# A delta-rule scan in chunks: the step's VectorE work replaced by precomputed transitions, and the tail moved into its own turn

## The chip, the cores and the metric

One core of a Trainium2 chip. The metric is the device time of one execution in microseconds (us), lower is better. TensorE (PE) multiplies, VectorE (DVE) and ScalarE (ACT) do the elementwise work, GpSimd (POOL) helps, SyncE (SP) issues most transfers. Each engine runs its own program in order and waits on semaphores for the others.

## The reference

`x` is [8, 256, 256] (batch, time, hidden), float32. It goes through a gated delta-rule attention layer with a residual and a layer norm, then through one ternary product with a residual and a layer norm:

```python
q = causal_dwconv_silu(x @ Wq.T, conv_wq).reshape(B, T, H, DK)      # H, DK, DV = 6, 32, 64
k = causal_dwconv_silu(x @ Wk.T, conv_wk).reshape(B, T, H, DK)      # depthwise, 4 taps
v = causal_dwconv_silu(x @ Wv.T, conv_wv).reshape(B, T, H, DV)
beta = jax.nn.sigmoid(x @ Wb.T)
g = -jnp.exp(A_log) * jax.nn.softplus(x @ Wa.T + dt_bias)
q = l2norm(q) * DK ** (-0.5)
k = l2norm(k)
def step(S, inp):                                   # scanned over time
    S = S * jnp.exp(gt)[..., None, None]
    v_new = vt - jnp.einsum('bhk,bhkv->bhv', kt, S)
    S = S + bt[..., None, None] * (kt[..., :, None] * v_new[..., None, :])
    o = jnp.einsum('bhk,bhkv->bhv', qt, S)
...
o = rmsnorm(o) * norm_w * jax.nn.silu(x @ Wg.T)     # per head
x = _layernorm(x + o @ Wo.T)
x = _layernorm(x + ternary(x) @ (ternary(weight) + rram_variation).T)
```

## The kernel before

The eight sequences are done as four pairs (`PAIRS`), one pair a turn. A pair has 12 heads (6 of each sequence); a tensor of 128 partitions holds four of them, so a pair has three groups (`G3`). The 256 time steps are cut in 8 chunks (`NC`) of 32 (`CH`); a unit is one group and one chunk, 24 (`U`) in a pair. All small products go through `by_head` (line 327): four 32x32 products, one for each head of a group, on four quarters of TensorE. Each float32 product shows as two MATMUL and two LDWEIGHTS in the trace; below, a pair of instructions is one load with its matmul, so one call of `by_head` is 8 pairs of instructions.

What a turn `k` does, and who does it:

- Front of the next pair `k + 1`. Six projections `project` (lines 334 to 346, two 128x128x512 products of hidden size each), copied out of PSUM by ACT (`tile_out_of_psum`, 608), three taps of the convolution on DVE (`conv_taps`, 910), Silu on ACT (`silu`, 621). Then `kq_to_tokens` (922), `square` (ACT, 654), `factors` (943: sums of squares, a reciprocal square root by three Newton steps, and the scales), `scaled_operands` (960), `v_to_tokens` (929), `exponents` (PE, 360), `exp_d` (ACT, 647), the mask `d_masked` on POOL (850), `chunk_products` (PE, 370) and `chunk_matrices` (DVE, 984). The triangular 32x32 matrices of the units are inverted: their 16x16 halves by `substitute(j)`, `j` = 1 to 14 (1006), turned by `inverse_to_rows` (1016), then joined by two products, `merge` and `merge_second` (382, 392) with the copy `merge_out` (669) between them, and `inverse` (1024) writes the result `t_t`.
- The scan of pair `k`, chunk by chunk. `from_state` (400) multiplies the state with keys and queries, DVE adds the values (`residual`, 1048), `solve` (417) multiplies with the inverse, ACT copies the result `u_sb` out of PSUM (`u_out`, 684), `to_state` (429) makes the new state's part and the output's, POOL scales the old state (`decay_state`, 862) and DVE adds the two (`next_state`, 1056). So one step passes PE, DVE, PE, ACT, PE and DVE. The PE program of a turn (510 to 553) puts a piece of the front or of the tail between the pieces of a step, and the DVE program (1224 to 1288) and the ACT program (743 to 791) do the same.
- The heads' norm and gate of pair `k` (`head_norm`, 1067; `gated`, 1096), at the end of the turn, with the three gate projections (`gates`, 348).
- The tail of the pair before, `k - 1`: the output projection (`project_out`, 446), the residual (`attention_sum`, 1117), the first layer norm (`first_norm`, 1127, and `normalize` on ACT, 714), the ternary values (`ternary`, 1134), their transposes and products (`feed_forward`, 458; `feed_forward_products`, 467), `feed_forward_sum` (1143), `moments` (1103), the second `normalize` and the store (`store`, 303).

The last turn has no front; it has the tail of pair 2 and, after the scan, the tail of pair 3 in two halves (the functions with `end_`, 1153 to 1222). PSUM has eight banks: `pj` (2), `fr` (3), `pc`, `po`, `pg`. `pc` takes every product of the scan's step.

```python
for c in range(NC):                       # DVE, lines 1226 to 1285, cut
    residual(k, c)
...
    next_state(k, c)
```

## Time and profile before

| | us |
|---|---|
| runs | 401.51, 403.58, 404.87, median 403.58 |
| the profiled execution | 404.34 |
| its span in the profile | 402.6 |
| DVE busy | 295.6 (73%) |
| PE busy | 260.4 (65%) |
| ACT busy | 131.7 (33%) |
| POOL busy | 33.1 (8%) |

The span runs from the first to the last instruction; what lies around it is the difference to the execution's time, 1.7 us. Busy time of PE is that of matmuls in a pipeline. Line numbers are those of the kernel above.

### The profile page before, as it was taken

How to read it: one execution, taken by the hardware profiler on the slowest of the kernel's cores; microseconds unless marked ns; L12 is line 12 of the kernel's file. 1: busy time of each engine (PE TensorE's matmuls, PEld its weight loads, DVE VectorE, ACT ScalarE, POOL GpSimd, SP SyncE). 2: the span in 40 equal slices, each digit the busy share in tenths (PEclk: the TensorE clock that was granted, in tenths of full speed). 3: DMA queues.
4: the chain of work that ended last, by engine and by line, in shares of the span. 5: the costliest groups of instructions: out<-in, count | busy, mean ns of one | idle time of the engine just before them, and what ended most of it. 6: DMA issues, size and time to landing. Idle time of an engine off the chain costs nothing.

```text
span 402.6 us, 13995 instructions
## 1 busy us (share of the span) xinstructions
PE 260.4 (65%) x6314; PEld 178.0 (44%) x6314; DVE 295.6 (73%) x756; ACT 131.7 (33%) x269; POOL 33.1 (8%) x44
## 2 busy tenths in 40 slices
PE   2993660479648558895566669866693375986641
PEld 1492430444545327463443455545542254654420
DVE  0664799927779895859798977697989654338996
ACT  0783401036732310566413214645022103134010
POOL 2000110001301000012110000103000001010000
PEclk9965585569968967999689589997697595899785
DMA  8500000000000010000000030000000420000001
GB/s 247 208 0 2 2 2 0 3 3 3 3 2 3 2 54 3 2 3 2 3 3 2 7 103 2 3 2 5 3 2 3 104 55 2 4 4 29 26 1 52
DMA packets 8012, 9.66 MB, mean 24 GB/s; under 512 B 1808, under 2 KB 7056, under 8 KB 7952
## 3 DMA queue, kind: packets, MB, share of 16 engines
q1 hardware_dynamic: 7024, 8.41, 6.6%
q8 instruction: 49, 0.80, 0.9%
q10 hardware_dynamic: 928, 0.36, 0.4%
q14 instruction: 11, 0.09, 0.1%
HBM read 6.67 MB, written 2.10 MB: 22 GB/s over the span
## 4 chain that ended last, share of the span: by engine, by line
DVE 46%; PE 27%; issue 8%; ACT 5%; DVEq 0%
PE pc L331 7%; DVE conv_buf L914 4%; PE pj L344 4%; PE pg L452 4%; PE fr L331 3%; DVE inv L1014 3%; DVE sub_buf L1012 3%; PE pg L356 3%; PE fr L475 2%; PE pj L452 2%; DVE stats L1106 2%; DVE r_sb L1053 2%; DVE conv_buf L1100 2%; DVE t_all L901 1%; DVE t_all L900 1%
## 5 line engine op out<-in xcount | busy, mean ns | idle before, releaser
L914 DVE SCALAR_TENSOR_TENSOR conv_buf<-raw,wconv,conv_buf 128x512 f32<-128x512 f32 x72 | 57.9, 810 | 16.9 <-ACT conv_buf L618 15.2
L344 PE MATMUL pj<-xt,wproj 128*128 128x512 f32 x96 | 54.0, 700 | 8.1 <-DMA xt<-x_t 7.4
L686 ACT ACTIVATE u_sb<-pc 128x192 f32<-128x192 f32 x32 | 10.5, 329 | 93.3 <-PE pc L331 93.3
L866 POOL TENSOR_TENSOR s_dec<-s_sb,decay 128x192 f32<-128x192 f32 x24 | 16.4, 683 | 278.2 <-DVE s_sb L1062 155.9
L331 PE MATMUL pc<-r_sb,t_t 32*32 32x64 f32 x672 | 16.5, 233 | 28.8 <-DVE r_sb L1053 28.0
L331 PE MATMUL fr<-x_t,x 32*32 32x16 f32 x768 | 11.6, 208 | 31.2 <-DVE x_t L1019 15.9
L344 PEld LDWEIGHTS pj<-xt,wproj 128*128 128x128 f32 x96 | 19.2, 218 | 26.9 <-issue 23.5
L331 PEld LDWEIGHTS pc<-r_sb,t_t 32*32 32x32 f32 x672 | 11.6, 113 | 39.3 <-DVE r_sb L1053 38.6
L452 PE MATMUL pg<-wout,conv_buf 128*128 128x256 f32 x36 | 14.6, 588 | 17.1 <-DVE conv_buf L1100 17.1
L331 PEld LDWEIGHTS fr<-x_t,x 32*32 32x32 f32 x768 | 10.9, 148 | 32.8 <-issue 32.8
L356 PE MATMUL pg<-xt,wproj 128*128 128x512 f32 x48 | 25.2, 648 | 0.0
L331 PE MATMUL pc<-s_sb,kc_ch 32*32 32x64 f32 x672 | 16.3, 231 | 11.1 <-DVE s_sb L1065 6.5
L331 PE MATMUL pc<-u_sb,kg_tok 32*32 32x64 f32 x672 | 17.1, 239 | 9.3 <-ACT u_sb L686 9.3
L331 PEld LDWEIGHTS pc<-u_sb,kg_tok 32*32 32x32 f32 x672 | 12.1, 117 | 21.4 <-ACT u_sb L686 11.9
L331 PEld LDWEIGHTS pc<-s_sb,kc_ch 32*32 32x32 f32 x672 | 11.8, 113 | 20.5 <-issue 10.9
L452 PEld LDWEIGHTS pg<-wout,conv_buf 128*128 128x128 f32 x36 | 10.8, 310 | 22.6 <-DVE conv_buf L1100 20.2
L331 PE MATMUL fr<-kq 32*32 32x64 f32 x768 | 20.3, 285 | 0.0
L693 ACT ACTIVATE o_all<-po 128x192 f32<-128x192 f32 x32 | 10.5, 328 | 29.8 <-PE po L331 29.6
L331 PE MATMUL po<-u_sb,a_t 32*32 32x64 f32 x768 | 18.7, 233 | 1.8 <-ACT u_sb L686 1.8
L331 PEld LDWEIGHTS fr<-kq 32*32 32x32 f32 x768 | 18.8, 155 | 1.2 <-issue 1.2
L1053 DVE TENSOR_TENSOR r_sb<-pc,v_tok 128x192 f32<-128x192 f32 x28 | 9.8, 351 | 10.6 <-PE pc L331 10.3
L1065 DVE TENSOR_TENSOR s_sb<-s_dec,pc 128x192 f32<-128x192 f32 x24 | 8.3, 348 | 12.5 <-PE pc L331 12.4
(162 smaller groups left out, 537.3 us busy)
## 6 DMA issues: line engine op xcount, KB each, us to landing
xt<-x_t SPq DMA_DIRECT2D x1, 1536.0 KB, 8.8
x_buf<-x SPq DMA_DIRECT2D x3, 512.0 KB, 4.2
out<-hid_buf SPq DMA_DIRECT2D x6, 256.0 KB, 4.5
wproj<-w_proj SPq DMA_DIRECT2D x1, 1024.0 KB, 8.0
xt<-x_t SPq DMA_DIRECT2D x1, 512.0 KB, 6.0
kq<-x SPq DMA_DIRECT2D x1, 512.0 KB, 3.5
out<-v_tok SPq DMA_DIRECT2D x2, 256.0 KB, 2.1
wout<-w_out SPq DMA_DIRECT2D x1, 384.0 KB, 9.6
```

The source lines that it names most:

```text
L331: mm = pe.matmul(out[rows], stationary[rows], moving[rows], **flags)
L344: mm = pe.matmul(pj[:, j % 2, :], wproj[:, t, j * P:(j + 1) * P], xt[:, t, k * TOK:(k + 1) * TOK], start=(t == 0), stop=(t == KT - 1))
L356: mm = pe.matmul(pg[:, :], wproj[:, t, w * P:(w + 1) * P], xt[:, t, k * TOK:(k + 1) * TOK], start=(t == 0), stop=(t == KT - 1))
L452: mm = pe.matmul(y_bank[part][:, (n % 2) * HID:(n % 2 + 1) * HID], o_ch[:, j, n * P:(n + 1) * P], wout[:, j, :], start=(j == 0), stop=(j = ...
L686: act.activation(u_sb[:, :, :].rearrange("p g v -> p (g v)"), pc[:, 0:G3 * DV], ACT.Copy).then_inc(u_done, 1)
L693: act.activation(o_all[:, :, c, :], po[:, 0:G3 * DV].rearrange("p (g v) -> p g v", g=G3), ACT.Copy).then_inc(o_out, 1)
L866: pool.tensor_tensor(s_dec[:, :, :], s_sb[:, :, :], decay[:, :, c:c + 1].to_broadcast([P, G3, DV]), ALU.mult).then_inc(sdec_done, 1)
L914: e = dve.scalar_tensor_tensor(out=conv[:, d, :, :], in0=raw[:, d, :, m:m + T], scalar=wconv[:, j, m:m + 1], in1=conv[:, d, :, :], op0=ALU ...
L1012: own(dve.tensor_tensor(step, columns[:, j:j + 1, :, 0:j].to_broadcast(grid), columns[:, j + 1:HALF, :, j:j + 1].to_broadcast(grid), ALU.m ...
L1014: own(dve.tensor_tensor(right, right, step, ALU.add))
L1053: dve.tensor_tensor(r_sb[:, :, :], pc[:, 0:G3 * DV].rearrange("p (g v) -> p g v", g=G3), v_tok[:, k % 2, :, c, :, :].rearrange("p g h v -> ...
L1065: dve.tensor_tensor(s_sb[:, :, :], s_dec[:, :, :], step, ALU.add).then_inc(s_done, 1)
```

## The change

- The scan's step. `solved` multiplies the inverse with keys and values of all 24 units at once (32x96 each, 192 pairs of instructions) and ACT copies the five banks out (`solved_out`). `transitions` multiplies, again for all units, the key part of that with `kga` (192 pairs), and DVE adds the decay on the diagonal and the scaled queries (`ad`) in three sums (`transition_sum`). After that a step is: `carried_state` (24 pairs), onto what `new_state` (24 pairs) has already put in the same PSUM bank, and one copy by ACT (`state_out`). `heads_out` makes the output from state and values (2 x 24 pairs). `residual`, `next_state`, `u_out` and POOL's `decay_state` are gone.
- The tail of a pair is done in the pair's own turn, after its gates, and before the inverse of the next pair is finished. A turn's `first_norm` moves with it; the second layer norm's square root is joined to that of `factors` in the next turn.
- Projections 0 to 3 of pair `k + 2` are made at the end of turn `k`, and 4 and 5 of pair `k + 1` in turn `k`.
- The mask of the exponents is added in PSUM by a bfloat16 product with -29952 above the diagonal, in place of POOL's `d_masked`; `park` and POOL's copy of the decay are gone.
- In the last turn both halves of the tail stand behind the scan on DVE.
- `o_ch` and the residual get memory of their own, and the residual is loaded as soon as the sums of the pair before have read it.

The core of the diff:

```diff
-        y_bank = (pg, pj[:, 1, :])
+        y_bank = (pc, po)
+        wu_bank = (pc[:, :], po[:, :], fr[:, 0, :], fr[:, 1, :], fr[:, 2, :])
+        s_bank = (pc, po)
+        o_bank = (pg[:, :], fr[:, 2, :])
...
+                for n in range(2):
+                    pe.matmul(pj[:, n, 0:UH * CH].rearrange("p (u t) -> p u t", t=CH), identb[:, :],
+                              negb[:, :].unsqueeze(1).to_broadcast([P, UH, CH]), start=True, stop=False)
...
+            def solved(k, b):
+
+                if b == 0:
+                    after(pe, tt_done, 1, k, 1)
+                    after(pe, kc_done, 1, k, 1)
+                    after(pe, v_tok_done, 1, k, 1)
+                    if not first(k):
+                        after(pe, y_in, 0, k, 2)
+                if b == 2 and not first(k):
+                    after(pe, ffn_in, 0, k, 2)
+                for n in range(b * WB, min(U, (b + 1) * WB)):
+                    c, g, i = n // G3, n % G3, n - b * WB
+                    mm = by_head(wu_bank[b][:, i * 96:(i + 1) * 96], t_t[:, g * NC + c, :], kr[:, c, g, :],
+                                 start=True, stop=True)
+                mm.then_inc(wu_mm, 1)
+
+            def transitions(k, b):
+
+                after(pe, wu_out, 3 + b, k, 5)
+                if b == 0:
+                    after(pe, kg_done, 1, k, 1)
+                    after(pe, at_done, 1, k, 1)
+                for n in range(b * MB, (b + 1) * MB):
+                    i = n - b * MB
+                    mm = by_head(fr[:, b, i * 64:(i + 1) * 64], wu[:, n, 0:DK], kga[:, k % 2, n // G3, n % G3, :],
+                                 start=True, stop=True)
+                mm.then_inc(mq_mm, 1)
...
+            def new_state(k, c):
+
+                if c < 2:
+                    after(pe, wu_out, c + 1, k, 5)
+                    after(pe, kg_done, 1, k, 1)
+                for g in range(G3):
+                    mm = by_head(s_bank[c % 2][:, g * DV:(g + 1) * DV], kga[:, k % 2, c, g, 0:DK],
+                                 wu[:, c * G3 + g, DK:], start=(g == 0), stop=(c == 0), skip_group_check=True)
...
+            def carried_state(k, c):
+
+                after(pe, s_done, c, k, NC - 1)
+                after(pe, mq_in, min(3, (c * G3 + 2) // MB + 1), k, 3)
+                if c == NC - 1:
                     return
...
+                    mm = by_head(s_bank[c % 2][:, g * DV:(g + 1) * DV], mq[:, c * G3 + g, 0:DK],
+                                 s_sb[:, c % 2, g * DV:(g + 1) * DV], start=False, stop=True, skip_group_check=True)
+                mm.then_inc(s_mm, 1)
...
+            def heads_out(k, c):
+
+                bank = o_bank[c // 2 % 2]
+                at = c % 2 * G3 * DV
+                if c == 0:
+                    after(pe, at_done, 1, k, 1)
+                if c == 2:
+                    after(pe, mq_in, 3, k, 3)
+                if c % 2 == 0 and c >= 4:
+                    after(pe, o_out, c // 2 - 1, k, NC // 2)
                 for g in range(G3):
...
+            def turn(k, front):
                 merge_second(k)
                 if front:
+                    project(k + 1, 4)
+                for b in range(5):
+                    solved(k, b)
+                new_state(k, 0)
+                heads_out(k, 0)
+                new_state(k, 1)
+                for b in range(3):
+                    transitions(k, b)
+                if front:
+                    project(k + 1, 5)
+                for c in range(1, NC):
+                    carried_state(k, c)
+                    if c < NC - 2:
+                        new_state(k, c + 1)
+                    heads_out(k, c)
+                    if not front and 1 <= c < 4:
+                        gates(k, c - 1)
+                if front:
+                    exponents(k + 1)
+                    for g in range(G3):
+                        chunk_products(k + 1, g)
+                    for j in range(GATE_TILES):
+                        gates(k, j)
+                    project_out(k, 0)
+                    project_out(k, 1)
+                    if not last(k + 1):
+                        project(k + 2, 0)
+                        project(k + 2, 1)
+                    feed_forward(k)
+                    if not last(k + 1):
+                        project(k + 2, 2)
+                    feed_forward_products(k, 0)
+                    feed_forward_products(k, 1)
+                    if not last(k + 1):
+                        project(k + 2, 3)
                     merge(k + 1)
...
+            def turn(k, front):
+                merge_out(k)
+                if front:
+                    silu(k + 1, 0)
+                    tile_out_of_psum(k + 1, 4)
+                solved_out(k, 0)
+                solved_out(k, 1)
+                if front:
+                    silu(k + 1, 1)
+                for b in range(2, 5):
+                    solved_out(k, b)
+                state_out(k, 0)
+                if front:
+                    silu(k + 1, 2)
+                    tile_out_of_psum(k + 1, 5)
+                for c in range(1, NC):
+                    if c < NC - 1:
+                        state_out(k, c)
+                    if c % 2:
+                        heads_out(k, c // 2)
+                    if front and c == 1:
+                        silu(k + 1, 3)
                     if front and c == 2:
                         square(k + 1)
                     if front and c == 3:
                         silu(k + 1, 4)
                     if front and c == 5:
+                        silu(k + 1, 5)
+                    if not front and 2 <= c < 5:
+                        gate_silu(k, c - 2)
+                    if not front and c == 4:
                         end_square(0)
+                    if not front and c == 5:
+                        normalize(k - 1, 1)
                 if front:
+                    exp_d(k + 1)
+                    if not first(k):
                         normalize(k - 1, 1)
+                    o_square(k)
+                    for j in range(GATE_TILES):
+                        gate_silu(k, j)
+                    upper_right(k + 1)
+                    if not last(k + 1):
+                        tile_out_of_psum(k + 2, 0)
+                        tile_out_of_psum(k + 2, 1)
+                    normalize(k, 0)
+                    ternary_out(k)
+                    if not last(k + 1):
+                        tile_out_of_psum(k + 2, 2)
+                        tile_out_of_psum(k + 2, 3)
                 else:
                     end_square(1)
...
+            def transition_sum(k, b):
+                after(dve, mq_mm, b + 1, k, 3)
+                after(dve, qe_done, 1, k, 1)
+                after(dve, decay_in, 1, k, 1)
+                units = slice(b * MB, (b + 1) * MB)
+                dve.tensor_tensor(mq[:, units, :].rearrange("p u x -> p (u x)"), fr[:, b, :],
+                                  ad[:, :, :, :].rearrange("p c g x -> p (c g) x")[:, units, :].rearrange(
+                                      "p u x -> p (u x)"), ALU.add).then_inc(mq_in, 1)
...
+            def turn(k, front):
+                head_eps(k)
                 if front:
+                    conv_taps(k + 1, 0)
+                inverse(k)
+                if front:
+                    for j in range(1, 4):
+                        conv_taps(k + 1, j)
+                else:
+                    rsqrt(r_n, v_n, t_n)
+                    shifts()
+                transition_sum(k, 0)
+                if front:
+                    kq_to_tokens(k + 1)
+                transition_sum(k, 1)
+                transition_sum(k, 2)
+                if not front:
+                    return
+                conv_taps(k + 1, 4)
+                conv_taps(k + 1, 5)
+                factors(k + 1, not first(k))
+                scaled_operands(k + 1)
+                v_to_tokens(k + 1)
+                head_norm(k)
+                chunk_matrices(k + 1)
+                gated(k)
+                for j in range(1, 7):
+                    substitute(j)
+                attention_sum(k, 0)
+                attention_sum(k, 1)
+                first_norm(k)
+                for j in range(7, 10):
+                    substitute(j)
+                ternary(k)
+                for j in range(10, HALF - 1):
+                    substitute(j)
+                inverse_to_rows(k + 1)
+                feed_forward_sum(k)
+                after(dve, ffn_in, 2, k, 2)
+                moments(hid)
```

## Rows read from the trace of the kernel before

**Rows 1.** Four turns: length; busy of PE, PEld, DVE, ACT, POOL; PEclk; DMA.

```profile
79.14:152.20 73.06, 49.74 (x1429) 31.66 (x1421) 56.94 (x125) 27.76 (x52) 7.60 (x9) 0.80 0.03 10
152.20:235.20 83.00, 58.02 (x1560) 38.96 (x1560) 67.80 (x161) 31.30 (x60) 8.44 (x9) 0.85 0.06 15
235.20:318.36 83.16, 56.20 (x1556) 39.31 (x1556) 67.86 (x162) 30.02 (x58) 8.44 (x9) 0.83 0.06 15
318.36:399.93 81.57, 53.53 (x1204) 38.28 (x1204) 50.95 (x186) 15.01 (x32) 3.06 (x6) 0.79 0.06 18
```

**Rows 2.** Waits of DVE, 221.84 to 305 us: total, times, longest.

```profile
DVE s_sb L1065 <- PE pc L331: 3.0, 3, 1.2
DVE hid_buf L1146 <- PE fr L475: 2.6, 2, 1.4
DVE hid_buf L1123 <- PE pg L452: 2.2, 1, 2.2
DVE hid_buf L1123 <- PE pj L452: 1.5, 1, 1.5
DVE v_tok L934 <- ACT x_buf L644: 1.5, 1, 1.5
```

**Rows 3.** Groups of DVE: busy us, mean ns; idle before.

```profile
L914 DVE SCALAR_TENSOR_TENSOR conv_buf<-raw,wconv,conv_buf 128x512 f32<-128x512 f32 x72 | 57.9, 810 | 16.9 <-ACT conv_buf L618 15.2
...
L1053 DVE TENSOR_TENSOR r_sb<-pc,v_tok 128x192 f32<-128x192 f32 x28 | 9.8, 351 | 10.6 <-PE pc L331 10.3
...
L958 DVE TENSOR_SCALAR norm_a<-norm,cst 128x24 f32<-128x24 f32 x4 | 2.6, 644 | 0.1
```

**Rows 4.** Stretches of DVE's work, columns as in rows 1.

```profile
302.36:306.81 4.45, 1.15 (x94) 1.02 (x98) 4.11 (x13) 1.81 (x2) 0.00 (x0) 0.98 0.00 0
280.33:290.69 10.36, 6.70 (x260) 6.30 (x252) 9.74 (x27) 0.99 (x3) 0.51 (x1) 0.66 0.01 4
370.18:399.93 29.75, 14.70 (x56) 9.95 (x56) 26.85 (x106) 2.48 (x5) 0.00 (x0) 0.69 0.08 27
```

**Rows 5.** PE in order of time, 72 to 84 us: start, length, idle before.

```profile
72.70 2.60 PE L331 MATMUL fr<-x_t,x 32*32 32x16 f32 x178 [15.87 <-DVE x_t L1019]
76.84 0.41 PE L331 MATMUL fr<-x_t,x 32*32 32x16 f32 x14 [1.53 <-issue]
77.94 1.69 PE L331 MATMUL fr<-x,p_sb 32*32 32x16 f32 x113 [0.69 <-ACT p_sb L673]
81.32 1.26 PE L331 MATMUL fr<-x,p_sb 32*32 32x16 f32 x79 [1.69 <-issue]
```

**Rows 6.** The page: busy time and instructions of the engines; queue of instruction packets.

```profile
PE 260.4 (65%) x6314; PEld 178.0 (44%) x6314; DVE 295.6 (73%) x756; ACT 131.7 (33%) x269; POOL 33.1 (8%) x44
...
q8 instruction: 49, 0.80, 0.9%
```

**Rows 7.** DMA of 72 to 84 us, in 40 slices of 0.3 us.

```profile
GB/s 0 0 0 0 0 0 0 55 0 0 0 0 0 0 0 0 0 0 0 0 0 0 0 55 0 0 0 0 0 0 0 0 0 0 55 0 0 0 0 0
```

**Rows 8.** PE in order of time, single products and projections.

```profile
227.74 3.78 PE L344 MATMUL pj<-xt,wproj 128*128 128x512 f32 x4
...
245.01 1.96 PE L344 MATMUL pj<-xt,wproj 128*128 128x512 f32 x4 [0.36 <-issue]
...
318.50 5.41 PE L452 MATMUL pg<-wout,conv_buf 128*128 128x256 f32 x12 [7.41 <-DVE conv_buf L1100]
...
361.02 0.54 PE L331 MATMUL pc<-u_sb,kg_tok 32*32 32x64 f32 x24 [0.45 <-ACT u_sb L686]
...
361.38 0.51 PE L331 MATMUL po<-u_sb,a_t 32*32 32x64 f32 x24
```

**Rows 9.** ACT in order of time.

```profile
228.21 2.07 ACT L719 ACTIVATE hid_buf<-hid_buf,shift,r_all 128x256 f32<-128x256 f32 x4 [6.59 <-DVE shift L1114]
...
271.88 0.87 ACT L650 ACTIVATE gm<-pj 128x384 f32<-128x384 f32 x2
...
303.28 1.48 ACT L710 ACTIVATE x_buf<-o_all 128x1536 f32<-128x1536 f32 x1
```

More of the change, by code:

```diff
@@ L587, in _ @@
             chunk_products(0, 0)
-            project(1, 0)
+            for j in range(AHEAD):
+                project(1, j)
             merge(0)
             pe.wait_ge(ld_wout, 16)
-            turn(0, True, False)
-            for k in range(1, PAIRS - 1):
-                turn(k, True, True)
-            turn(PAIRS - 1, False, True)
+            for k in range(PAIRS):
+                turn(k, not last(k))
             end_project_out(0)
@@ L823, in _ @@
             upper_right(0)
-            turn(0, True, False)
-            for k in range(1, PAIRS - 1):
-                turn(k, True, True)
-            turn(PAIRS - 1, False, True)
+            for j in range(AHEAD):
+                tile_out_of_psum(1, j)
+            for k in range(PAIRS):
+                turn(k, not last(k))
             for s in range(2):
@@ L1327, in _ @@
             dve.wait_ge(beta_in, 24)
[L1328 to L1329 removed]
+            factors(0, False)
             scaled_operands(0)
```

521 lines of the change are left out of this document (150 added, 371 removed).

## The prediction

> **What bounds the kernel now.** I read the turns first [rows 1]: turns 1 and 2 last 83.0 and 83.2 us, with VectorE (DVE) busy for 67.8 of it and TensorE (PE) for 56 to 58; turn 0 lasts 73.1, and the last turn with the end 81.6. Then what DVE waits for in such a turn [rows 2]: the five largest groups are 10.8 us, every one for a product of PE or a copy of ACT, and two smaller ones add 1.1. So a turn is 83.2 - 11.9 = 71.3 us of DVE's own program (small bubbles between dependent instructions included), and the rest is waiting for the other two. DVE is the bound, with PE close behind.
>
> The reader should then look at the rate at which PE gets its instructions. Two merges of 192 pairs stand back to back [rows 5]. 178 pairs run in 2.6 us, then PE idles 1.53 us with "issue" as the reason; 14 + 113 = 127 pairs later it idles again, 1.69 us. The page has 49 packets and 0.80 MB in an instruction queue, against 2 x 6314 = 12,628 instructions of PE [rows 6]: 258 instructions or 129 pairs a packet, which is the distance of the two stalls. The packets fall at slices 7, 23 and 34 of 0.3 us [rows 7], near 74.1, 78.9 and 82.2 us; the stalls end at 76.84 and 81.32, 2.4 to 2.7 us after the first two packets. So where small products stand close, a packet of 128 pairs takes 3.3 us (third packet minus second) to 4.8 us (second minus first), 26 to 37 ns a pair. When instructions are there, 24 pairs of 32x64 start 0.36 us apart, 15 ns a pair [rows 8]. In turn 2 the 1556 pairs [rows 1] are 12.2 packets in 83 us, mostly spaced by the scan's own waits, and the shortage costs little. I take 3.7 us a packet, nearer to the shorter gap, since the longer one holds a 0.69 us wait for ACT.
>
> **The change, part by part.**
>
> *DVE's work in a steady turn.* Out: 14 instructions of the scan (7 `residual`, 7 `next_state`), 0.35 us each [rows 3], 4.9; the copy of `park`, at most 0.35 like them, 0.3. In: three sums of 128x512, priced as a tap of the same size, 0.81 each [rows 3], 2.4. The diagonal product in `scaled_operands` takes the place of a transpose of the same size: 0, give or take 0.2. Strided writes to `kr`, `kga` and `ad`: not shown by the trace, between 0 and 1 us a turn; I take 0. Work: 71.3 - 4.9 - 0.3 + 2.4 = 68.5.
>
> *PE's program.* Pairs a turn in the scan: before 37 groups of 24 = 888. After: `solved` 192, `transitions` 192, `new_state` 7, `carried_state` 6, `heads_out` 15 groups of 24 = 672; 1056 in all, 168 more. With both merges and `chunk_products` (192 each) small products are 1632 pairs a turn, 12.8 packets, and 1248 of them stand in one stretch with only one projection inside. At 15 ns that stretch is 18.7 us (a 32x96 product a little more, at most half as much again: +1.4), at 3.7 us a packet 36.
>
> *Waits of DVE in a steady turn*, in the order of its new program:
> - The inverse. `ternary` ends; then in a row on PE and ACT: transposes 1.0 at the low clock, `project(k+2,2)` 3.8 at the low clock after PE's idle stretch [rows 8], products 3.2, `project(k+2,3)` 1.9, both merges. The merges take 9.9 us in rows 5 (72.70 to 82.58); here the first has its packet, I take 8.5. Sum 18.4. DVE does beside it: substitutions 10 to 14 and two transposes 4.5 [rows 4]; two sums, `moments`, three taps and the first product, estimated at 6.4 from their sizes against the tap's 0.81. Wait 7.5. The transposes' and feed-forward products' times are estimates too, by their columns against the projection's.
> - The transitions. After the second merge: projection 1.9, then 328 pairs until the first `transition_sum` (192 + 72 + 64): 5.6 us at 17 ns, 9.5 at 3.7 a packet; with part of it loaded I take 7.9. DVE beside: rest of the inverse 1.2, three convolutions 6.9 (three taps are 3 x 0.81 less what overlaps). Wait 1.9.
> - `square` behind the first steps, and the last Silu: 1.5 together, an estimate; 0 if ACT is free.
> - `head_norm`. From the first transitions: 128 + 600 pairs, 5.7 packets, 21.1 us (10.9 at 15 ns); exponents and mask on PE 2.0 (4 x 384 columns against a projection's 4 x 512, plus the mask); then on ACT the exponent 0.9, `normalize(k-1, 1)` 2.1 and the squares 1.5 [rows 9], which stand in that order in its program: 27.6. DVE beside: sums 2.4, two convolutions of three taps 4.6, `factors` and `scaled_operands` 10.1 (less one scan instruction [rows 4]), the transposes of keys, queries and values 3.6 by their size, the waits above 1.5: 22.2. Wait 5.4.
> - `project_out`. It now starts when `gated` ends, PE having idled before: 5.4 us [rows 8] against six substitutions at 0.5 to 0.6 (five of them and two transposes are the 4.45 us of rows 4), 3.3, is 2.1; the second half at the full clock, half of 5.4, against one sum, 0.7, is 2.0. Together 4.1, and 0.2 for the hand-overs.
> - `normalize` ahead of `ternary` 2.1 [rows 9], beside it three substitutions, 1.8: 0.3.
>
> Sum 20.9; turn 68.5 + 20.9 = 89.4, against 83.1. Without a limit by packets the same list gives about 3.2 + 0 + 0 + 2.3 + 4.3 + 0.3 = 10.1, a turn of 78.6: the merges take 4.3 less (2 x 1.8 to 2.8), the stretch from the transitions on 10 less, of which DVE's own work then hides most. (The clock of the first merge decides 1 us each way.)
>
> *Turn 0* has no `normalize(-1, 1)` (-2.1) and its inverse is not waited for at the start (-4): 83.3, against 73.1, in which no tail stood. The waits added on PE (`gates` for the whole scan, `merge_second` for `xqt_done`) queue only work that nobody awaits earlier.
>
> *The last turn.* Inverse late by 4.3, then 6 us of inverse and square root; `solved` to `transitions` is 456 pairs, 13.3; four steps of the scan with three gate projections inside, 13; squares 0.8: the first half's sums start 33.7 us after the turn's start. From there DVE runs to the end without a wait: the second half's chain took 29.8 us [rows 4], and the first half adds the same head work once more, 8.0 (it lay beside the scan before): 37.8. Together 71.5, against 81.6.
>
> *Before turn 0*: the turn starts at 79.1. `norm_a` of pair 0, a 128x24 instruction, ran beside POOL's `d_masked`; the four of them took 2.6 us [rows 3] where such an instruction takes 0.2, so I put 1.6 to that and take it off. Transfers: the residual's load moves ahead on SP, the stores wait as before; 0.
>
> Sum: 77.5 + 83.3 + 2 x 89.4 + 71.5 = 411.1; from DVE's last instruction to the end of the span 402.6 - 399.9 = 2.7 [rows 1] and 1.7 around the span as before: 415.5. The profiled execution took 404.3, 0.8 above the median of 403.6, so against the median this is a little high; I forecast 415.
>
> *A rule against this.* The Trainium skill, "Runtime: NRT & Kernel Launch", section "Instruction fetch mechanics", says that instructions come in blocks of 256, fetched ahead of need, and that the fetch is mostly hidden because the sequencer issues more slowly than blocks arrive. The trace agrees on the block and not on the hiding, as rows 5 and 7 show. By the rule the result would be rival A.
>
> **Rivals.**
> - *A: the packets keep up* (PE's sequencer runs far enough ahead in the long stretch). Turns of 79, 78.6 twice and 61.5 (scan 10 us shorter): 77.5 + 79 + 157.2 + 61.5 + 4.4 = 380. For it: in the steps at 361 us [rows 8] no issue stall is in sight. Against: rows 5, and a denser program than any stretch of before. This one ends on the other side; it holds if a packet takes less than 2.6 us.
> - *B: a packet takes 3.3 to 3.45 us.* Every 0.1 us a packet is worth 12.8 packets, some three quarters of them on the path, four turns: 3.5 to 4 us. At 3.4 us: 415 - 11 = 404, no change.
> - *C: a packet takes 4.1 us* (the mean of the two gaps in rows 7): 415 + 15 = 430.
> - *D: the scan is as slow as before for another reason:* each step waits for ACT's copy behind Silu and squares. A step's chain is 0.54 (products [rows 8]) and ACT's copy, under 0.9; a Silu or the squares hold ACT 1.5 us at most [rows 9]. Two such in each of three turns come to +6 at most: 421, within the range. Against it: with 96 pairs a step the packets alone take 2.8 us, longer than either.
>
> **How the numbers follow.** Forecast with D (407 to 424) 0.50; C and beyond (over 424) 0.15; B (396 to 407) 0.17; A (under 396) 0.18. The bounds of strided writes (+3) and of the merge's clock (3 either way) are inside. What can be told from no change is about 1%, 399.5 to 407.6. Faster: A and a fifth of B, 0.21; same: the rest of B, 0.13; slower 0.66. Range 392 to 434.
>
> **What would show it.** Right: turns of about 89 us; PE idling with "issue" as reason in the stretch of `solved`, `transitions` and steps; DVE waiting for the merge 4 to 8 us a turn and for the heads' squares 4 to 6 us; some 54 to 56 packets, spaced 3.4 to 4.5 us in that stretch; the last turn's scan far shorter than before. Wrong: no issue stalls and a stretch from `solved` to the last step of under 20 us (then A), DVE's work above 70 us a turn, or a turn 0 shorter than 80 us.

## The result, and the profile after

Before took 403.0 us (median of 4), after 416.9 in the profiled execution, a ratio of 1.029 (1.023 to 1.036): the change makes the kernel slower. Of the four timed runs of after (411.9, 416.9, 421.2 and 421.5 us) the two that lie over 1.5% above the fastest are left out of the ratio as disturbed, so it rests on two runs. Below, "after" is 1.0293 x 402.7 = 414.5 us, where 402.7 is the time of before beside the experiments (402.6 to 402.9). "Measured" gives a kernel's median and its ratio, and distances between kernels go by the ratios, in the same way. The span is 415.1 us against 402.6. The stretches between the starts of VectorE's turns, columns as in [rows 1]:

```profile
75.80:161.76 85.96, 58.87 (x1622) 41.60 (x1618) 64.34 (x148) 30.85 (x56) 1.48 (x1) 0.83 0.03 9
161.76:250.82 89.06, 58.48 (x1750) 41.08 (x1740) 64.46 (x148) 33.28 (x61) 1.48 (x1) 0.85 0.05 15
250.82:339.87 89.05, 54.62 (x1799) 41.35 (x1788) 64.55 (x148) 29.08 (x54) 1.48 (x1) 0.79 0.03 9
339.87:412.40 72.53, 45.76 (x1305) 35.11 (x1304) 39.97 (x149) 13.01 (x27) 0.00 (x0) 0.74 0.07 21
```

Against [rows 1], DVE works 3.3 us less in a steady turn and the turn is 6 us longer; turn 0 is 12.9 longer, the last turn with the end 9.0 shorter. The waits of DVE in turn 1 (161.76 to 250.82; total, times, longest) stand where [rows 2] stood:

```profile
DVE m_o L1056 <- ACT x_buf L731: 7.6, 1, 7.6
DVE t_t L1036 <- PE pg L329: 4.7, 1, 4.7
DVE mq L1046 <- PE fr L329: 2.7, 3, 2.3
DVE hid_buf L1105 <- PE po L484: 1.8, 1, 1.8
DVE hid_buf L1128 <- PE fr L507: 1.8, 2, 1.1
DVE hid_buf L1105 <- PE pc L484: 1.4, 1, 1.4
```

With 1.3 us of smaller ones they are 21.3 us, so DVE's own program is 89.1 - 21.3 = 67.8, 3.5 less than before, and its waits are 9.4 more. The chain has turned round: PE 46% and DVE 28% of it, "issue" 15%, where DVE had 46, PE 27 and "issue" 8. PE in order of time in the same turn (start, length, idle before), from the end of the second merge to the exponents:

```profile
168.38 0.82 PE L329 MATMUL pg<-x,p_sb 32*32 32x16 f32 x43 [2.48 <-issue]
169.14 3.78 PE L340 MATMUL pj<-xt,wproj 128*128 128x512 f32 x4
...
181.01 1.91 PE L329 MATMUL fr<-kga,wu 32*32 32x64 f32 x121 [1.48 <-issue]
182.85 1.98 PE L340 MATMUL pj<-xt,wproj 128*128 128x512 f32 x4
...
191.52 0.25 PE L329 MATMUL fr<-wu,kga 32*32 32x64 f32 x4 [1.85 <-issue]
...
195.50 0.54 PE L329 MATMUL po<-s_sb,mq 32*32 32x64 f32 x24 [2.00 <-issue]
...
199.39 0.43 PE L329 MATMUL fr<-wu,kga 32*32 32x64 f32 x16 [1.90 <-issue]
...
200.85 0.82 PE L364 MATMUL pj<-negb,identb 128*128 128x384 bf16 x2
```

In the steps PE starts again after a stop every 3.9 to 4.0 us (191.52, 195.50, 199.39), having stood for 1.85 to 2.00 us with nothing that the profile shows to wait for. The instruction packets fall in step with it. Bytes in 40 slices of 0.6 us, 184 to 208 us:

```profile
GB/s 0 0 27 0 0 0 0 27 0 0 0 0 0 0 27 14 0 0 0 0 0 27 0 0 0 0 0 27 0 0 0 0 0 0 0 27 0 0 145 292
```

They stand 5 to 8 slices apart, 3.0 to 4.8 us, on the mean (35 - 2) / 5 = 6.6 slices or 4.0 us. From the waits of PE over the whole span, after:

```profile
PE fr L329 <- issue: 20.9, 12, 4.0
PE pg L329 <- issue: 14.5, 11, 2.5
PE po L329 <- issue: 8.9, 6, 2.0
PE pc L329 <- issue: 3.0, 2, 2.0
```

47.3 us, where the kernel before has 17.1 in one row of this kind and 1.0 in two more. The page's rows that answer to [rows 6] and [rows 3]:

```profile
PE 262.5 (63%) x6994; PEld 187.3 (45%) x6994; DVE 283.4 (68%) x718; ACT 138.2 (33%) x269; POOL 8.5 (2%) x14
...
q8 instruction: 55, 0.90, 1.0%
...
L915 DVE SCALAR_TENSOR_TENSOR conv_buf<-raw,wconv,conv_buf 128x512 f32<-128x512 f32 x72 | 53.1, 750 | 17.3 <-ACT conv_buf L642 15.6
```

### The profile page after: what moved, and what is told of

It reads as the page before. It is cut to its first block, busy times and chain, and to the rows that moved or that the text cites. A ratio compares the mean times of both kernels' runs of the same rounds, so it can differ in the third digit from the quotient of the medians.

```text
span 415.1 us, 15255 instructions
## 1 busy us (share of the span) xinstructions
PE 262.5 (63%) x6994; PEld 187.3 (45%) x6994; DVE 283.4 (68%) x718; ACT 138.2 (33%) x269; POOL 8.5 (2%) x14
## 4 chain that ended last, share of the span: by engine, by line
PE 46%; DVE 28%; issue 15%; ACT 8%; DMA 2%; DVEq 0%; SPq 0%; ACTq 0%
PE pj L340 11%; PE fr L329 9%; PE pg L329 5%; PE pc L329 4%; PE pc L484 3%; PE po L329 3%; PE fr L507 3%; PE fr L593 2%; PE po L484 2%; DVE r_all L895 2%; DVE t_all L894 2%; DVE t_all L893 2%; DMA xt<-x_t 2%; PE pj L354 2%; DVE o_ch L1082 2%
## 5 line engine op out<-in xcount | busy, mean ns | idle before, releaser
L641 ACT ACTIVATE raw<-pj 128x512 f32<-128x512 f32 x24 | 14.3, 598 | 79.9 <-PE pj L340 79.7
L484 PE MATMUL pc<-wout,o_ch 128*128 128x256 f32 x36 | 14.0, 566 | 34.0 <-DVE o_ch L1082 34.0
L484 PEld LDWEIGHTS pc<-wout,o_ch 128*128 128x128 f32 x36 | 10.5, 301 | 38.8 <-DVE o_ch L1082 36.4
L329 PE MATMUL pg<-x,p_sb 32*32 32x16 f32 x768 | 10.6, 196 | 12.4 <-issue 11.7
L1056 DVE TENSOR_REDUCE m_o<-x_buf 128x24 f32<-128x1536 f32 x3 | 5.3, 1753 | 18.6 <-ACT x_buf L731 18.6
L329 PE MATMUL fr<-kga,wu 32*32 32x64 f32 x768 | 12.7, 215 | 7.8 <-issue 7.8
L495 PE MATMUL pg<-identb,tok_buf 128*128 128x128 bf16 x24 | 3.1, 311 | 21.2 <-DVE tok_buf L1122 21.2
L642 ACT ACTIVATE conv_buf<-pj,wconv 128x512 f32<-128x512 f32 x24 | 16.4, 684 | 0.0
L329 PEld LDWEIGHTS fr<-kga,wu 32*32 32x32 f32 x768 | 11.5, 105 | 8.5 <-issue 8.5
L1017 DVE TENSOR_TENSOR inv<-inv,sub_buf 128x28 f32<-128x28 f32 (+6 forms) x56 | 13.7, 244 | 1.9
L1015 DVE TENSOR_TENSOR sub_buf<-inv 128x28 f32<-128x28 f32 (+6 forms) x56 | 13.6, 242 | 1.6
L329 PE MATMUL fr<-kq 32*32 32x64 f32 x768 | 12.9, 222 | 1.1 <-issue 1.1
L668 ACT ACTIVATE kq<-conv_buf 64x256 f32<-64x256 f32 (+1 forms) x24 | 11.6, 483 | 4.8 <-DVE conv_buf L915 4.7
L1140 DVE TENSOR_REDUCE m_o<-raw 128x12 f32<-128x768 f32 x2 | 1.9, 950 | 15.1 <-ACT raw L752 15.1
```

Source lines behind the costliest of these rows:

```text
L329: mm = pe.matmul(out[rows], stationary[rows], moving[rows], **flags)
L484: mm = pe.matmul(y_bank[part][:, (n % 2) * HID:(n % 2 + 1) * HID], o_ch[:, j, n * P:(n + 1) * P], wout[:, j, :], start=(j == 0), stop=(j = ...
L641: act.activation(raw[:, SLOT[j], :, TAPS - 1:], bank, ACT.Copy)
L642: act.activation(conv[:, SLOT[j], :, :], bank, ACT.Identity, scale=wconv[:, j, TAPS - 1:TAPS]).then_inc(tile_out, 1)
L668: e = act.activation(dst, conv[rows, SLOT[j], src, :], ACT.Silu)
L1015: own(dve.tensor_tensor(step, columns[:, j:j + 1, :, 0:j].to_broadcast(grid), columns[:, j + 1:HALF, :, j:j + 1].to_broadcast(grid), ALU.m ...
```

## The experiments

The expectations of tiny_extra, large_extra, one_for_four and act_order start from 419 us, the median of all four runs of after; the others from 415. A "stall" is idle time of PE with "issue" as its reason.

**More small products, and more large ones.** tiny_extra puts a product on 8 columns ahead of each one of `solved` and `transitions`:

```diff
+                    by_head(wu_bank[b][:, i * 96:i * 96 + 8], t_t[:, g * NC + c, :], kr[:, c, g, 0:8],
+                            start=True, stop=True)
                     mm = by_head(wu_bank[b][:, i * 96:(i + 1) * 96], t_t[:, g * NC + c, :], kr[:, c, g, :],
```

> Before every small product of the solved rows and of the transitions stands one more on the first 8 columns of the same place, with the same operands; the full product writes over it. 48 x 4 float32 products, 384 pairs of PE a turn, in which little is computed. Supply theory (a packet of 128 pairs takes about 3.8 us in this stretch and sets its pace): 3 packets a turn, 11.4 us, nearly all on the way to the transition sums and the heads' squares, 12 packets in all: 419 + 40 = 459 (450 to 465), q8 with 67 packets in place of 55. PE-time theory (a pair costs the 15 ns at which pairs start when they are there): 1536 x 15 ns = 23, at most 442. ACT or DVE theory (copies, their order, DVE's own work): DVE hides it, 419 to 425.

Measured: 465.9 us, ratio 1.159 (1.152 to 1.166), 67 packets: 52 us above after, 34 ns for each of the 1536 pairs, where a pair takes 15 ns when it is there. PE's time alone would be 23 by that price, and nearer 12, since a pair on 8 columns takes only 8 ns (worked out from a line of tiny_before, below). So most of the 52 us is not PE's own work, and nothing of it is hidden behind DVE.

large_extra repeats the last projection three times in its place:

```diff
-                for t in range(KT):
+                for t in [t for _ in range(4 if j == 5 and not first(k) else 1) for t in range(KT)]:
                     mm = pe.matmul(pj[:, j % 2, :], wproj[:, t, j * P:(j + 1) * P],
```

> In turns 0 to 2 the last projection of the next pair is computed four times in place of once, in the same place between the transitions and the steps: 3 x 1.96 = 5.9 us more of PE a turn by the full-clock duration, but only 12 pairs more, a tenth of a packet. PE-time theory: 3 x 5.9 = 17.6, so 436. Supply theory: packets go on arriving behind the large products, and the stalls after them get shorter: 0 to 3 us a turn, 419 to 428. ACT or DVE theory: the squares are waited for 5.9 us longer as well, 436. What the copies of the large products leave out: nothing, the result stands in the same place.

Measured: 434.3, ratio 1.079 (1.073 to 1.085), 20 us above after. That is what the PE-time theory said, and my picture of packets that go on arriving behind large products is wrong. Its large products, and the same view of the packets, 184 to 208 us of this kernel:

```profile
191.39 7.13 PE L340 MATMUL pj<-xt,wproj 128*128 128x512 f32 x16
...
GB/s 0 27 0 0 0 0 0 27 14 0 0 0 0 0 27 0 0 0 0 0 0 0 0 0 0 0 0 0 27 0 0 0 0 0 27 0 14 0 0 0
```

From slice 14 to 28, 8.4 us, none comes (the 14 in slice 8 is of another queue). My reading was that the supply is one packet ahead and no more: a packet in which a projection stands has next to no stall to give (1.8 us of small products and 1.96 of projection are one packet's time; after stalls 0.49 us behind its own), and what is added to it is paid in full. That became the theory of the runs that follow, "one packet ahead".

spread_extra holds the same three copies, one each behind the groups 1 and 3 of `solved` and ahead of `transitions`:

```diff
                 for b in range(5):
                     solved(k, b)
+                    if b in (1, 3):
+                        once_more()
                 new_state(k, 0)
                 heads_out(k, 0)
                 new_state(k, 1)
+                once_more()
```

> The same three further copies of the last projection as in large_extra (turns 0 to 2, 5.9 us of PE a turn, 12 pairs), but one at a time: behind the second and the fourth group of the solved rows and ahead of the transitions, so that each falls into another packet's 128 pairs of small products. Theory 'one packet ahead' (the next packet is asked for when the last one is entered, and takes about 3.8 us; 128 small pairs take 1.9, so each packet of small products alone has 1.9 us of stall, and a packet that already holds a projection has none): the copies mostly fall into stalls, 0 to 2.5 us a turn, 415 to 423, against the 434 of large_extra, where all three stand in one packet that had no stall left. PE-time theory: 434 as in large_extra. Nothing left out.

Measured: 428.2, ratio 1.059 (1.051 to 1.067): 8 us below large_extra by the ratios, for the same work, but 12 above after where at most 8 were expected. The direction is that of "one packet ahead", the size is not. Its timeline shows why: in this part of the stretch after had one stall only, the 1.48 us above, since `project(k+1,4)`, 3.78 us at the low clock, stands just ahead. The copies found little to fill, and the stalls of 1.6 to 1.7 us in the steps behind them stayed.

**Fewer instructions.** one_for_four takes one product with a 128x128 stationary operand for the four heads:

```diff
+            def as_one(out, stationary, moving, **flags):
+                return pe.matmul(out, cst[:, C_IDENT:C_IDENT + P], moving, **flags)
```

> In the solved rows, the transitions and the steps of the scan, one product with a 128x128 stationary operand stands in place of the four 32x32 ones of the heads (1056 pairs a turn become 264, 6.2 packets less). The stationary operand is the identity, so the scan's mathematics is left out; operands of the other side, places, waits, ACT's copies and DVE's sums are the same. PE's own time stays near: 64 columns x 4 passes / 2.4 GHz = 0.11 us for each, against 8 x 15 ns = 0.12. Supply theory: the stretch loses 6.2 x 3.8 = 24 us of its pace and DVE's own work takes over: waits for the transitions and the squares nearly gone, last turn some 12 shorter: 419 - 35 = 384 (375 to 392). PE-time theory: no change, 415 to 422. ACT or DVE theory: no change, 415 to 422.

Measured: 426.9, ratio 1.062 (1.056 to 1.069), 30 packets: slower than after, and all theories missed. The kernel leaves the scan's mathematics out. The assumption on PE's time was wrong:

```profile
187.24 0.83 PE L333 MATMUL pc<-wu,cst 128*128 128x64 f32 x6
187.91 0.83 PE L333 MATMUL pg<-wu,cst 128*128 128x64 f32 x6
```

Six such pairs start 0.67 us apart from the next six, 0.111 each, against 0.36 for the 24 small ones they replace. No stall stands between them, and the stretch from `project(k+1, 4)` to the exponents is now PE's own work: 264 x 0.111 + 3.8 + 2.0 = 35.1, measured 35.6. So the run does not decide between the theories; it says that 128-row products are no way out here.

bf16_scan halves the pairs in another way, by the type of the operands (a float32 product is two pairs, a bf16 product one):

```diff
-        kr = sb("kr", [P, NC, G3, DK + DV])
+        kr = sb("kr", [P, NC, G3, DK + DV], BF16)
```

and so `kga`, `mq`, `wu`, `t_t`, `s_sb` and `v_ch`.

> The operands of the solved rows, the transitions and the steps (solved rows, keys, values, products on the transitions, carried state) are stored as bf16, so that each product is one pair of weight load and product in place of two: 1056 pairs a turn become 528, 4.1 packets less. ACT's copies and DVE's sums keep their sizes. Supply theory: up to 4.1 x 3.8 = 15.7 us less on PE's way from the inverse to the last step, of which DVE's waits for transitions and squares give back 7 to 9 a turn in turns 0 to 2 and 10 to 13 in the last: 415 - 35 = 380 (372 to 392), q8 near 39 packets. PE-time theory (pair at 15 ns, half of them gone): 7.9 us less on the same way, 415 - 25 = 390; so this run tells supply and PE's time apart only by the stalls in its timeline. ACT or DVE theory: 412 to 418. The scan is computed with bf16 operands, which is less exact; sums stay float32.

Measured: 383.8, ratio 0.949 (0.943 to 0.956), 32 us below after and faster than both kernels. In the steps PE now waits for something else:

```profile
173.19 0.26 PE L330 MATMUL pc<-wu_buf,kga 32*32 32x64 bf16 x12
173.27 0.26 PE L330 MATMUL pg<-wu_buf,kga 32*32 32x64 bf16 x12
...
177.48 0.35 PE L330 MATMUL pc<-s_sb,mq 32*32 32x64 bf16 x12 [1.02 <-ACT s_sb L709]
...
181.95 0.34 PE L330 MATMUL fr<-wu_buf,kga 32*32 32x64 bf16 x12 [1.61 <-ACT s_sb L709]
```

These are the copies of the state behind ACT's other work, rival D of the prediction; it comes to the surface when the scan's packets are half as many. The run does not tell supply from PE's time: not only are the pairs half as many, each is shorter too. Twelve of them start 0.08 us before the next twelve at 173.19, 7 ns a pair and not the 15 that the expectation's PE-time theory took, so that theory would have given more than 25 us as well. Its stalls over the span are 27.7 us against 47.3.

**The supply by itself.** A kernel without the layer's work, of small products with large ones set between them, profiled once:

```diff
+                    mm = pe.matmul(bank[rows, 0:64], src[rows, 0:32], src[rows, 64:128], start=True, stop=True)
+                    if larges and i % 64 == 31:
+                        wide_product(larges)
```

> The kernel's work is left out; PE runs five stretches of small float32 products (32x32 by 32x64, 1280 pairs each), apart from each other by eight 128x512 products: with no large product inside, with one, two or four 128x512 float32 products (0.98 us each at the full clock) after every 64 small products (128 pairs), and one stretch of 1280 pairs in bf16. Theory 'one packet ahead, 3.8 us each': per 128 small pairs 3.8 us with none, 3.8 with one, 3.9 with two, 5.9 with four; bf16 3.8 as well. Theory 'packets run ahead without limit while PE is busy with large products': the first packets after the eight large ones would come without a stall, and two per 128 pairs would show none. PE-time theory: 1.9, 2.9, 3.9, 5.9, bf16 under 1.9.

PE in order of time. With no large product inside, right behind sixteen large pairs:

```profile
18.79 3.10 PE L137 MATMUL none<-small 32*32 32x64 f32 x207
22.95 1.99 PE L137 MATMUL none<-small 32*32 32x64 f32 x128 [1.07 <-issue]
26.68 1.99 PE L137 MATMUL none<-small 32*32 32x64 f32 x128 [1.74 <-issue]
30.14 1.99 PE L137 MATMUL none<-small 32*32 32x64 f32 x128 [1.47 <-issue]
...
47.68 1.99 PE L137 MATMUL none<-small 32*32 32x64 f32 x128 [1.47 <-issue]
```

From 22.95 to 47.68 are seven packets, 3.53 us each for 128 pairs that run in 1.92. At the start 207 pairs were there: the rest of one packet and the one ahead, however long the large products had taken. With one large product, and with two, after every 128 pairs:

```profile
86.15 0.42 PE L137 MATMUL one<-small 32*32 32x64 f32 x15 [0.80 <-issue]
86.50 1.13 PE L128 MATMUL large<-xs 128*128 128x512 f32 x2
87.56 1.76 PE L137 MATMUL one<-small 32*32 32x64 f32 x111
90.15 0.46 PE L137 MATMUL one<-small 32*32 32x64 f32 x17 [0.83 <-issue]
...
108.61 1.98 PE L128 MATMUL large<-xs 128*128 128x512 f32 x4
110.53 1.99 PE L137 MATMUL two<-small 32*32 32x64 f32 x128
112.44 1.98 PE L128 MATMUL large<-xs 128*128 128x512 f32 x4
...
211.98 2.30 PE L137 MATMUL half<-smallb 32*32 32x64 bf16 x259
216.41 1.21 PE L137 MATMUL half<-smallb 32*32 32x64 bf16 x128 [2.12 <-issue]
...
223.32 1.89 PE L137 MATMUL half<-smallb 32*32 32x64 bf16 x128 [1.56 <-issue]
227.32 1.90 PE L137 MATMUL half<-smallb 32*32 32x64 bf16 x128 [2.11 <-issue]
```

With one, a round takes 4.00 us (90.15 - 86.15; over seven rounds 3.92) and still stalls 0.8; with two 3.83 and no stall; with four 5.55 and none, all work. In bf16 it is 3.45 to 4.00 us for 128 pairs, though these run in 1.2 us at 216.41 (granted clock 1.0) and in 1.9 later (0.5): the price of a packet is by instruction, not by type or clock. The run agrees with "one packet ahead" at 3.5 to 4.0 us a packet, and with neither of the others, with one correction. 259 pairs of the bf16 stretch ran without a stall, 3 more than two packets. By the DMA view a packet came at 205.6 us, while the sixteen large pairs had just begun, and the next at 213.9, 2.5 us before the stall ended. So the packet "being run" is the one that PE's sequencer is in, and that can be some tens of pairs ahead of the products. Here the Trainium skill, "Runtime: NRT & Kernel Launch", section "Instruction fetch mechanics", which has the fetch mostly hidden, holds for the stretches with two or more large products a packet and not for the others.

**Undoing parts.** fewer_pairs takes back the 168 pairs that the change adds a turn, by leaving out the carried state's part of the outputs:

```diff
-                if c > 0:
-                    for g in range(G3):
-                        mm = by_head(bank[:, at + g * DV:at + (g + 1) * DV], mq[:, c * G3 + g, DK:],
-                                     s_sb[:, c % 2, g * DV:(g + 1) * DV], start=False, stop=True,
-                                     skip_group_check=True)
```

> The changed kernel without the second product of the heads' outputs (the carried state on its transition) in chunks 1 to 7: 7 groups of 24, 168 pairs of PE a turn less, which brings its count to that of the kernel before. Left out is the carried state's part of the outputs; waits, copies and places stay. Supply theory (one packet ahead, 3.5 to 3.9 us for 128 small pairs): 1.3 packets, 4.6 to 5.1 us a turn on PE's way to the squares, in turns 0 to 2 nearly all of it on the path, in the last turn about half: 415 - 17 = 398 (394 to 402). PE-time theory: 168 x 15 ns = 2.5 a turn, 415 - 9 = 406. If the loss comes from where things are placed and not from the number of pairs: 412 to 416.

Measured: 403.6, ratio 0.999 (0.995 to 1.002): 12 us below after, 18 ns a pair, between the two theories' sums and nearer to neither (at 15 ns the 672 pairs alone are 10 us). It says where the loss is, though: with the pairs of before, the change costs nothing. It does not say how much of the loss is supply and how much is the pairs' own time.

tiny_before puts 360 pairs a turn into the old scan, as tiny_extra did with 384 into the new one:

```diff
+                    by_head(pc[:, g * DV:g * DV + 8], t_t[:, g * NC + c, :],
+                            v_tok[:, k % 2, g, 0, 0, 0:8] if c == 0 else r_sb[:, g, 0:8], start=True, stop=True)
```

> The kernel before with one more product on the first 8 columns ahead of each product of the solve and of the state's update (15 groups of 24, 360 pairs a turn, against 384 in tiny_extra), which the full product writes over. Each group lengthens its step's chain by 24 x 15 ns = 0.36 us: 15 x 0.36 = 5.4 a turn, 21.6 in all, and that is PE's time alone, 424. If supply costs what tiny_extra's 51 us show wherever pairs stand: 403 + 48 = 451. Theory 'one packet ahead': a step of 6 to 7 us has 120 small pairs and large products between waits, and takes 168 small pairs with some of the longer fetch hidden: 424 to 435. Nothing left out.

Measured: 416.7, ratio 1.035 (1.030 to 1.041): 14 us, 10 ns a pair against 34 ns in the changed kernel, and below every expectation, PE's time of 21.6 too. That 21.6 was priced too high, as a group of this kernel with its 24 added pairs on 8 columns shows:

```profile
255.87 0.73 PE L331 MATMUL pc<-u_sb,kg_tok 32*32 32x8 f32 x48
256.42 0.51 PE L331 MATMUL po<-u_sb,a_t 32*32 32x64 f32 x24
```

The 48 pairs take 0.55 us where 24 took 0.36 [rows 8], so an added pair takes 8 ns, and the 1440 of them 11.5 us. In the old chain small pairs cost little beyond their own time, and its stalls did not grow (16.3 us against 18.1). In the changed kernel the same kind of pair costs four times its own time.

bf16_before gives the old scan the same operands as bf16_scan:

```diff
-        u_sb = sb("u_sb", [P, G3, DV])
+        u_sb = sb("u_sb", [P, G3, DV], BF16)
```

and so `kc_tok`, `kc_ch`, `qe_tok`, `qe_ch`, `kg_tok`, `a_t`, `t_t`, `r_sb`, `s_sb`, `v_ch` and `v_tok`.

> The kernel before with the operands of its scan in bf16 (keys and queries by channels, values, inverse, residual, updated values, state; sums stay float32): 888 pairs a turn become 444. If the supply of instructions is what turns the change into a loss, the kernel before, whose steps are spaced by their own chain of PE, ACT and DVE, gains little from half the pairs: each of 37 groups ends 12 x 15 ns = 0.18 us earlier, some 22 of them on the chain, 4 us a turn at most and DVE's work unchanged: 403 - 8 = 395 (390 to 400), against 384 of the changed kernel with the same operands; the change is then worth 11 us where instructions are cheap. If the gain of bf16_scan comes from bf16 itself (DVE, ACT, copies), this one falls as far: 403 - 31 = 372.

Measured: 396.3, ratio 0.984 (0.977 to 0.991): 6 us gained, where the changed kernel gains 32. In float32 the change costs 12 us, in bf16 it is worth 0.984 - 0.949 of 402.7, 14, more than the 11 expected.

**The order on ACT, the place of a projection, and the best kernel.**

```diff
-                    if not first(k):
-                        normalize(k - 1, 1)
                     o_square(k)
+                    if not first(k):
+                        normalize(k - 1, 1)
```

> ACT's program in turns 1 and 2 has the squares of the heads ahead of the output's normalization (four activations, 2.07 us) instead of behind it. Every theory in which DVE waits for the squares on the path expects 2.1 us less in each of two turns, if the exponents (and not the normalization) end the copy before it: 419 - 4 = 415. If PE's late products are what the squares wait for and the normalization fits before the last copy, 0. Nothing left out.

Measured: 412.4, ratio 1.023 (1.016 to 1.030): 2.5 us below after, inside both intervals. DVE's waits for the squares fall from 18.6 to 14.1 us in the profiles; that this reaches the end is not shown.

```diff
             def turn(k, front):
+                if front and not first(k):
+                    project(k + 1, 3)
                 merge_second(k)
```

and the two copies out of PSUM behind `merge_out(k)` on ACT.

> On top of act_order: in turns 1 and 2 the fourth projection of the next pair stands between the two merges (beside ACT's copy of the first) and no longer ahead of both, and its two copies out of PSUM stand behind ACT's copy of the merge. PE's sum of work is the same. Theory 'one packet ahead': one more packet of small products has a large one inside, up to 1.9 us less of stall and 0.7 us of waiting for ACT covered in each of two turns: 412 - 4 = 408 (406 to 411). PE-time theory: only the covered wait for ACT, 411. If ACT's later copies hold up VectorE's fourth convolution: 412 to 414. Nothing left out.

Measured: 408.3, ratio 1.010 (1.005 to 1.015): 7.7 below after, and the intervals are apart, so the gain of both edits together is shown. The second one's share is open: the profiled spans of the two kernels are 406.6 and 407.1, and PE's "issue" idle is 48.7 us against 47.7, not less, so the reason I gave for it has nothing to stand on.

> bf16_scan and late_project together (the scan's operands in bf16; the heads' squares ahead of the output's normalization on ACT; the fourth projection between the merges). The merges stay float32 and dense, so that what late_project gave there is still to be had; the squares' 2.07 us a turn are to be had if DVE still waits for them. 384 - 5 = 379 (376 to 382). If DVE is the bound by now and the waits are gone: 384.

Measured: 377.3, ratio 0.935 (0.929 to 0.942), with the edits of bf16_scan and late_project: the fastest here, 26 us below before; its scan is less exact than the float32 one. Its turns 1 and 2, columns as in [rows 1]:

```profile
154.72:233.45 78.73, 48.34 (x1180) 30.25 (x1179) 64.01 (x149) 31.67 (x59) 1.48 (x1) 0.78 0.05 16
233.45:312.77 79.32, 43.98 (x1252) 28.77 (x1253) 63.93 (x148) 29.02 (x55) 1.68 (x1) 0.76 0.03 9
```

These turns are as long as the 78.6 us that the prediction gave for a scan without a limit by packets, with DVE busy for 64 of it. The likeness is in the number: this kernel still stalls for 23.0 us, and its pairs are shorter.

**One stretch in all kernels.** From the start of `project(k+1, 4)` to the exponents in turn 1, by the timelines: pairs in it, length, and length by packet of 128.

| kernel | pairs | us | us a packet |
|---|---|---|---|
| fewer_pairs | 896 | 28.1 | 4.0 |
| after | 1064 | 31.7 | 3.8 |
| tiny_extra | 1448 | 44.4 | 3.9 |
| spread_extra | 1076 | 35.6 | 4.2 |
| large_extra | 1076 | 37.0 | 4.4 |
| bf16_scan | 536 | 19.6 | 4.7 |
| one_for_four | 272 | 35.6 | 16.8 |

The first three, which differ only in small products, lie on one price. Their own work, at 15 ns a pair (8 ns for those on 8 columns) with two projections (3.8 + 2.0), would be 19, 22 and 25 us. In the last two packets are not what sets the length.

## Why the prediction was right, point by point

- *The rate of packets* was the number on which all rested: 3.7 us taken, from two gaps of 3.3 and 4.8 in [rows 7]. Alone it is 3.53, in the steps 3.9 to 4.0, over the stretch 3.8. Rival A (380) fell with it. No run here takes the limit away and leaves the float32 scan as it is; that bf16_scan comes to 384 does not confirm A's sum, for its pairs are fewer and shorter.
- *DVE's work in a steady turn*: 68.5 forecast, 67.8 measured. The sums cost 0.69 instead of 0.81, and the taps fell from 810 to 750 ns, for which I had nothing. The trace of before has the reason. 13 of its 72 taps overlap an instruction of POOL and take 1.09 us on the mean, up to 2.17; the other 59 take 0.75, and so do all 72 of after, none of which overlaps one. Three taps alone, three beside POOL, and POOL's products:

```profile
184.73 2.31 DVE L914 SCALAR_TENSOR_TENSOR conv_buf<-raw,wconv,conv_buf 128x512 f32<-128x512 f32 x3
...
189.27 3.87 DVE L914 SCALAR_TENSOR_TENSOR conv_buf<-raw,wconv,conv_buf 128x512 f32<-128x512 f32 x3
...
189.43 0.95 POOL L866 TENSOR_TENSOR s_dec<-s_sb,decay 128x192 f32<-128x192 f32 x1 [5.97 <-DVE s_sb L1065]
190.35 2.25 POOL L854 TENSOR_TENSOR dt_m<-gm,cst 128x768 f32<-128x768 f32 x1
```

Side by side both are longer: elsewhere in the same turn POOL's 128x192 product takes 0.51 us and one of 128x768 takes 1.48. No run takes POOL's work alone away, but the overlaps account for all long taps. With that work gone the taps of turn 1 fell from 15.1 to 13.5 us, 1.6 that the forecast lacks; with it and the cheaper sums the forecast would have been 66.5, and what makes up the other 1.3 us is not worked out. Strided writes cost nothing that shows.
- *Waits in turns 1 and 2*: inverse 7.5 forecast, 6.5 and 4.3 measured; transitions 1.9, 2.7 and 4.8; squares of keys, Silu and the tile's copy 1.5, 0.8 and 2.4; heads' squares 5.4, 7.6 and 5.7; `project_out` 4.3, 3.2 and 3.5; ternary 0.3, 0.5 and 0.5. The sum is 20.9 against 21.3 and 21.2, the turn 89.4 against 89.1 twice. The places were right; the single sizes are off by up to 3 us and make up for each other, since what one wait leaves the next one takes: PE's way from the merge to the squares is one chain.
- *Turn 0*: 83.3 forecast, 86.0 measured, the worst term. Its waits are 18.1 us and not 14.8: the transitions 4.0 in place of 1.9, and the heads' squares 5.3 in place of 3.3; ACT waited there for PE's late exponents (0.75 us at 116.2) before it could make them.
- *The last turn with the end*: 71.5 forecast, 72.5 measured. The half's squares were summed at 374.6, with the turn's start at 339.9 that is 34.8 after it, against 33.7; from there to DVE's end (412.4) 37.8, as forecast. The 33.7 does not follow from the terms that stand before it: 4.3, 6, 13.3, 13 and 0.8 are 37.4. Measured are 6.9 to the end of the inverse, 12.0 from there to the last transition and 15.9 to the squares' sums.
- *Before turn 0*: the turn starts at 75.8, 3.3 us earlier and not 1.6. `norm_a` took 0.24 us and not 1.86, which is the 1.6. The rest is not the taps, which take 0.75 us there in both kernels: DVE's copies into `par` begin 1.2 us earlier (40.71, before 41.92), for a reason that is open, and the copy to `park` with its gap is 0.4.
- *The sum*: 75.8 + 86.0 + 2 x 89.1 + 72.5 + 2.7 + 1.8 = 417.0, the profiled execution; forecast 415.5, with +2.7 in turn 0 and +1.0 in the last turn against -1.7 ahead of them and -0.6 in turns 1 and 2. The path is right; that the sum comes within 1.5 us is partly luck. Of the signs named, the turns of 89 us, the stalls, 55 packets and the shorter last turn came. Others came only in part: the wait for the merge was 4.7 us in turn 1 but 1.9 in turn 2, the heads' squares 7.6 in turn 1 where 4 to 6 were named; and single packets came 3.0 to 4.8 us apart where 3.4 to 4.5 were named.
- *What the prediction had half right*: it priced the packets as a mean along the stretch. The runs show that the price hangs on what else stands in a packet, and where the pairs stand: 168 pairs a turn were worth 12 us and not 17 to 20, and 384 were worth 52.
- *Rival D* is hardly in the float32 kernel: PE waits 2.6 us over the whole span for the copies of the state (`s_sb`), against 47.3 of "issue". In bf16_scan it shows.

## What to carry to other kernels

Count PE's instructions by stretch, not only its time. On this chip a stretch of small products costs the greater of its own work and some 3.5 to 4.0 us for every 128 load-and-product pairs; a chain of waits between small groups hides the part beyond their own work (14 us for 1440 added pairs in tiny_before), a dense program doesn't (52 us for 1536 in tiny_extra), and so taking waits out of a scan can be worth less than the pairs it adds. Put large products one by one between small ones, where stalls are, and try a type with half the pairs before the order is tuned: bf16 operands gained 32 us here, moving a projection and the squares 7.7.

## What the runs showed of the hardware that was not expected

- The instruction supply of PE holds one packet beyond the one being run and asks for the next no earlier: 8.4 us without a packet while 7.1 us of large products ran, and 207 float32 or 259 bf16 pairs without a stall behind sixteen large ones. The second number is over two packets, so the sequencer was ahead of the products.
- A 128x128 by 128x64 float32 pair takes 0.111 us, so four heads as one product cost 0.223 us in two pairs against 0.12 us in eight, when these are there.
- A lower granted clock went with a faster kernel: 0.74 in bf16_late at 377 us, 0.80 in after.
- A float32 pair of 32x32 by 32x64 takes 15 ns, one on 8 columns 8 ns and a bf16 one 7 ns in bf16_scan and 9 in supply_alone, all at a granted clock of 1.0; a packet of 128 costs 3.5 to 4.0 us in supply_alone in either type.
- VectorE's taps beside products of GpSimd took 1.09 us on the mean, up to 2.17, and 0.75 without them.
